# Tokens normalized, turned and copied in two halves, residual sums kept in PSUM, the last up slabs in two strips, in an eight-layer graph and feed-forward kernel

## The chip, the core and the metric

The kernel runs on one core of a Trainium2 chip. The metric is the device time of one execution in microseconds; the time of a kernel is the median of its runs. TensorE (PE) multiplies matrices into PSUM, VectorE (DVE) and ScalarE (ACT) work elementwise, GpSimd (POOL) does small work, and SyncE (SP) issues most of the transfers.

## The reference

128 tokens of 768 float32 values pass through eight layers, each of which adds to x what it computes of the normalized x:

```python
x = x + gnn0(_layernorm(x), src, dst)      # graph attention, two layers
x = x + ffn0(_layernorm(x))                # routed attention, mixing, then a small MLP on a second norm
x = x + gnn1(_layernorm(x), src, dst)
x = x + moe1(_layernorm(x))                # mixture of 8 experts, 2 per token, and a shared one
x = x + gnn2(_layernorm(x), src, dst)       # graph attention with a relu behind it
x = x + moe2(_layernorm(x))                # 8 small experts, all resident
x = x + gnn3(_layernorm(x), src, dst)
x = x + moe3(_layernorm(x))                # mixture of 8 experts, 2 per token
return x

def _layernorm(x, axis=-1, eps=1e-05):
    m = jnp.mean(x, axis=axis, keepdims=True)
    v = jnp.var(x, axis=axis, keepdims=True)
    return (x - m) / jnp.sqrt(v + eps)
```

The lines of the layers are shortened here. One expert is `silu(x @ Wg.T) * (x @ Wu.T) @ Wd.T`.

## The kernel before

All tokens lie on the 128 partitions, so every layer is a sequence of products with the tokens (turned, 128 x 128 a tile, six tiles) as the stationary side, while weights stream past. The weights come as 271 slabs of 128 x 3072 float32 (1.5 MB) through 14 slots; SP issues each slab as its slot's previous one has been used. Each engine has its instructions in an order written out by hand, and semaphores tie them. A queue is worked strictly in order, so a wait holds everything behind it.

Stages in order: `first_wide(0)` and `second(1)` (graph 0), the FFN0 code, `first_narrow(2)` and `second(3)` (graph 1), `mixture(1)`, the attention 2 and its feed-forward, `first_narrow(5)` and `second(6)` (graph 3), `mixture(3)`. Between stages stands a joint; there are nine, with the number `i` of `layernorm`/`layernorm_affine` (L973, L986). Joints 4 and 8 lead into the mixtures, joint 5 out of the first, joint 2 is the second norm within FFN0 (on H1), joints 6 and 7 surround the small experts. A joint runs so:

- TensorE leaves a layer's result in PSUM bank pair AC (768 columns, written as 512 and 256 by `halves()`), and raises x_product.
- VectorE's `take_x` (L1210) adds it to X in SBUF, takes two `bn_stats` of 384 columns, aggregates, adds epsilon; GpSimd (L639) raises to the power -0.5; VectorE normalizes into XN (L979).
- TensorE's `turn` (L1499) transposes six tiles into TP. ScalarE's `transposed` (L677, `transposed_hi` L681) copies 768 columns to XT (or XTh), and the next products start. Where a fp32r split is used, VectorE makes the low part (L1089, L1104).
- `keep_warm(n)` (L1494) is n products of the identity with itself, whose result nobody reads; some stand ahead of each turning.

In `mixture` (L1745 on TensorE), AC is first started with identity times X, so that the experts' results add to it. The router picks experts; VectorE writes their order (L1302), and only then can SP read the numbers of the experts and load their slabs (L576). A pass is a 512-wide slice of one expert (full, split in high and low parts by ScalarE L856 and VectorE L1276) or of two experts side by side (pair, one slab for each side). It does up g (gate), the turning of the pass before, up u, then down of the pass before (L1798, L1851, L1860). The last three passes of mixture 3 (48 to 50) are pairs, as those of mixture 1 (15 to 17). `STRIPS` (L184) loads the down slabs of the last two passes in 2 and 4 strips with a semaphore each. Ahead of g and of u in the last pass stand `keep_warm(14)` (L1930, L1945). At the end VectorE copies X out of AC.

Of the kernel before, what the change touches and what calls it, by code (L numbers as in the profile page):

```python
# [30 lines left out]
E8 = 8  # L31
# [152 lines left out]
STRIPS = {LAST_PASS[l] - back: parts for l in (1, 3) for back, parts in ((1, 2), (0, 4))}  # L184


def strips_of(n):

    l, q, kind, side = WEIGHTS_OF.get(n, (0, 0, "", 0))
    return STRIPS.get(q, 1) if kind == "d" else 1  # L190
# [90 lines left out]
def gnn_ffn_kernel(nc, x_in, edges_in, weights, rows_in, cols_in, small_in, attn_in, ffn0_vectors, l2_terms_in, out):  # L281
    with ExitStack() as ctx:
# [47 lines left out]
        stats = sb("stats", [P, 2, 6])  # L330
# [159 lines left out]

        def group(c, g):
# [46 lines left out]
        def _(sp):  # L538
# [11 lines left out]
            def mixture(l, static_slots, segments, vectors):  # L550
# [3 lines left out]
                for n in range(m["slab"], m["slab"] + 9 * (3 * m["per"]) - (0 if m["shared"] else 3 * m["per"])):  # L554
# [27 lines left out]
                    q, parts = WEIGHTS_OF[n][1], strips_of(n)  # L582
# [3 lines left out]
                    for t in range(parts):  # L586
                        part = slice(t * SLAB // parts, (t + 1) * SLAB // parts)
                        for of, index in closing:
                            sp.dma_start(slab_at(of)[:, part], weights[index, :, part]) \
                                .then_inc(S(f"strip_landed_{q}_{t}"), 16)  # L590
# [83 lines left out]
        def _(act):  # L674
            A = nc.scalar.activation

            def transposed(k):  # L677
                act.wait_ge(S("tr_product"), k + 1)
                A(XT[:].rearrange("p k n -> p (k n)"), TP[:, 0:D], ACT.Copy).then_inc(S("tr_ready"), 1)

            def transposed_hi(k):  # L681

                act.wait_ge(S("tr_product"), k + 1)
                A(XTh[:].rearrange("p k n -> p (k n)"), TP[:, 0:D], ACT.Copy).then_inc(S("tr_ready"), 1)
# [136 lines left out]
            def mixture(l):  # L821
# [38 lines left out]
                A(XTh[:].rearrange("p k n -> p (k n)"), TP[:, 0:D], ACT.Copy).then_inc(S("XTh_ready"), 1)  # L860
# [29 lines left out]
            transposed_hi(0)  # L890
            first_wide(0)
            second(1)

# [8 lines left out]
            act.wait_ge(S("tr_product"), 3)  # L902
            A(MIXT.rearrange("p k n -> p (k n)"), PJ[:, 0:D], ACT.Copy).then_inc(S("mix_ready"), 1)
# [22 lines left out]

            transposed(4)
            first_narrow(2)
            second(3)
            mixture(1)  # L930

            act.wait_ge(S("l2_v_product"), 1)
# [20 lines left out]
            A(CBT[0:E8, :], TP[0:E8, SEG:SEG + P], ACT.Copy).then_inc(S("l2_T_ready"), 1)  # L953

            transposed_hi(8)
            first_narrow(5)
            second(6)
            act.wait_ge(S("graph_used"), GRAPH_HALVES)
# [4 lines left out]
        def _(dve):  # L963
# [9 lines left out]
            def layernorm(i, src, dst, sem=None, count=0):  # L973
# [5 lines left out]
                last = v.tensor_scalar(dst, src, mv[:, 0:1], rstd[:, 0:1], ALU.subtract, ALU.mult)  # L979
                if sem is None:  # L980
                    then(last)
                else:
                    last.then_inc(S(sem), 1)
                    dve.wait_ge(S(sem), count)

            def layernorm_affine(i, src, gain, offset):  # L986

                v.bn_stats(stats[:, 0, :], src[:, 0:384])
                then(v.bn_stats(stats[:, 1, :], src[:, 384:768]))
                then(v.bn_aggr(mv[:], stats[:]))  # L990
                if i == 1:
# [3 lines left out]
                else:  # L995
                    v.tensor_scalar(veps[:, 0:1], mv[:, 1:2], LN_EPS, None, ALU.add).then_inc(S("ln_variance"), 1)
                then(v.scalar_tensor_tensor(XN[:], src, mv[:, 0:1], gain, ALU.subtract, ALU.mult))
                dve.wait_ge(S("ln_rstd"), i + 1)
                v.scalar_tensor_tensor(XN[:], XN[:], rstd[:, 0:1], offset, ALU.mult, ALU.add) \
                    .then_inc(S("tr_input"), 1)  # L1000
# [85 lines left out]
            def transposed_lo(k):  # L1086

                dve.wait_ge(S("tr_ready"), k + 1)
                v.tensor_tensor(XTl[:].rearrange("p k n -> p (k n)"), TP[:, 0:D],  # L1089
                                XTh[:].bitcast(F32).rearrange("p k n -> p (k n)"), ALU.subtract) \  # L1090
                    .then_inc(S("XTl_ready"), 1)
# [8 lines left out]

            def graph_tokens_lo():

                dve.wait_ge(S("tr_ready"), 8)
                v.tensor_tensor(XT_lo.rearrange("p k n -> p (k n)"), TP[:, 0:D],  # L1104
                                XTh[:].bitcast(F32).rearrange("p k n -> p (k n)"), ALU.subtract) \
                    .then_inc(S("graph_tokens_lo"), 1)
# [102 lines left out]

            def take_x(n, add, relu=False):  # L1210

                dve.wait_ge(S("x_product"), n - (n > 4))
                if relu:
                    ins = v.scalar_tensor_tensor(X[:], AC[:, 0:D], 0.0, X[:], ALU.max, ALU.add)
                else:
                    ins = v.tensor_tensor(X[:], AC[:, 0:D], add, ALU.add)
                ins.then_inc(S("x_ready"), 1)
                dve.wait_ge(S("x_ready"), n)
# [1058 lines left out]
```

## Time and profile before

| | us |
|---|---|
| median of 3 runs | 1235.09 (1233.28 to 1235.66) |
| the profiled execution | 1234.37 |
| its span | 1232.4 |
| PE busy | 1169.4 |
| DVE busy | 569.2 |
| ACT busy | 440.3 |
| transfers | 443.15 MB, mean 360 GB/s |

The span runs from the first to the last recorded instruction; the execution's time is a little longer. Busy time of TensorE includes products on constants. The view by stretches gives for each stretch the busy time of each engine, then TensorE's granted clock as a share of full speed, the share in which the DMA engines were busy and what they moved. The timeline lists instructions by start with what ended the idle time before them; the chain lists what the end of the span goes back to. A float32 product appears as two matmul records.

### The profile page before, as it was taken

Reading aid. Unit: us, or ns where it says so; the run is one execution under the profiler, and the core shown is the slowest. Engines: PE = TensorE matmul, PEld = TensorE weight load, DVE = VectorE, ACT = ScalarE, POOL = GpSimd, SP = SyncE. Lnnn points to the kernel's source line nnn. Section 1 sums busy time; section 2 is a strip of 40 time slices with the busy share of each in tenths; the row PEclk is TensorE's granted clock in tenths of the full one; section 3 lists DMA queues with packets and bytes.
Section 4 is the critical chain, followed back from the end, with each engine's and each line's share of the span. In section 5 each row is a group of like instructions: output and inputs, shape, how many; then the busy total and the mean of one; then the engine's idle time right before and its main releaser. Section 6 shows DMA issues by size and latency. Waiting matters only on the chain.

```text
span 1232.4 us, 16004 instructions
## 1 busy us (share of the span) xinstructions
PE 1169.4 (95%) x6537; PEld 744.7 (60%) x6537; DVE 569.2 (46%) x870; ACT 440.3 (36%) x494; POOL 22.0 (2%) x47
## 2 busy tenths in 40 slices
PE   5999999889999999999999999999999999889998
PEld 4677785667855455545866776575565655445543
DVE  6977632337644234301556575463554533233310
ACT  4765512224633223201434345353443422222210
POOL 2000000000000000000000000000000000000000
PEclk9999999999999999999899999999999999999999
DMA  9988645944999999999457498999999999999996
GB/s 376 423 357 346 229 184 208 416 158 190 388 420 424 426 425 426 425 421 420 179 192 277 161 404 307 426 426 426 425 425 425 425 425 426 426 424 424 426 426 247
DMA packets 44647, 443.15 MB, mean 360 GB/s; under 512 B 5008, under 2 KB 5168, under 8 KB 10784
## 3 DMA queue, kind: packets, MB, share of 16 engines
q1 hardware_dynamic: 41760, 427.05, 83.8%
q0 software_dynamic: 2816, 15.09, 3.2%
q8 instruction: 52, 0.85, 0.3%
q14 instruction: 19, 0.16, 0.0%
HBM read 441.73 MB, written 0.39 MB: 359 GB/s over the span
## 4 chain that ended last, share of the span: by engine, by line
PE 78%; DMA 11%; DVE 6%; ACT 3%; issue 1%; POOL 0%; SPq 0%; DVEq 0%; ACTq 0%
PE PJ L1847 17%; DMA scratch<-in_weights 10%; PE PJ L1819 10%; PE AC L1884 8%; PE TP L1906 8%; PE PJ L1828 5%; PE AC L1643 3%; PE MS L1497 3%; PE AC L1655 3%; PE TP L1857 2%; PE PJ L1810 2%; PE PJ L1603 1%; DMA ring<-in_weights 1%; PE PJ L1556 1%; PE PJ L1558 1%
## 5 line engine op out<-in xcount | busy, mean ns | idle before, releaser
L1847 PE MATMUL PJ<-scratch,picked 128*64 128x512 f32 (+1 forms) x564 | 144.5, 595 | 0.5 <-DMA scratch<-in_weights 0.5
L1906 PE MATMUL TP<-ring,extra 128*64 128x512 f32 (+3 forms) x720 | 118.0, 488 | 1.9 <-issue 1.9
L1258 DVE SCALAR_TENSOR_TENSOR act<-low,CB,PJ 128x512 f32<-128x512 f32 x51 | 38.0, 746 | 167.7 <-PE PJ L1847 84.1
L839 ACT ACTIVATE low<-PJ 128x512 f32<-128x512 f32 x51 | 30.2, 592 | 230.0 <-PE PJ L1847 157.6
L1276 DVE TENSOR_TENSOR ring_lo<-ring,w_hi_u 128x1536 fp32r<-128x1536 f32 x46 | 79.6, 1756 | 69.2 <-ACT w_hi_u L856 69.1
L1847 PE MATMUL PJ<-ring,picked 128*32 128x512 f32 (+1 forms) x456 | 101.6, 594 | 0.0
L856 ACT ACTIVATE w_hi_u<-ring 128x1536 fp32r<-128x1536 f32 x46 | 66.9, 1484 | 57.8 <-PE AC L1884 27.1
L1276 DVE TENSOR_TENSOR ring_lo<-ring,w_lo_u 128x1536 fp32r<-128x1536 f32 x40 | 68.9, 1754 | 37.6 <-ACT w_lo_u L856 37.6
L1906 PEld LDWEIGHTS TP<-ring,extra 128*64 128x64 f32 (+1 forms) x720 | 46.7, 126 | 61.5 <-issue 52.9
L1828 PE MATMUL PJ<-ring_lo,XTh 128*128 128x512 f32 x198 | 77.9, 394 | 0.0
L1847 PEld LDWEIGHTS PJ<-scratch,picked 128*64 128x64 f32 (+1 forms) x564 | 42.2, 125 | 55.7 <-issue 55.0
L856 ACT ACTIVATE w_lo_u<-scratch 128x1536 fp32r<-128x1536 f32 x32 | 46.8, 1484 | 77.8 <-DMA scratch<-in_weights 53.0
L856 ACT ACTIVATE w_lo_u<-ring 128x1536 fp32r<-128x1536 f32 x40 | 57.8, 1483 | 31.7 <-PE AC L1884 19.4
L1497 PE MATMUL MS<-ident 128*128 128x128 f32 x566 | 68.8, 276 | 0.0
L1497 PEld LDWEIGHTS MS<-ident 128*128 128x128 f32 x566 | 66.1, 192 | 2.5 <-issue 2.1
L1819 PE MATMUL PJ<-w_lo_u,extra_lo 128*128 128x512 f32 x150 | 61.0, 407 | 0.0
L1819 PE MATMUL PJ<-w_hi_u,extra_lo 128*128 128x512 f32 x150 | 59.3, 406 | 1.2 <-DVE ring_lo L1276 1.2
L1819 PE MATMUL PJ<-w_lo_u,XTh 128*128 128x512 f32 x150 | 59.0, 393 | 0.0
L1819 PE MATMUL PJ<-w_hi_u,XTh 128*128 128x512 f32 x150 | 59.0, 393 | 0.0
L1847 PE MATMUL PJ<-extra,picked 128*64 128x512 f32 (+1 forms) x132 | 58.6, 593 | 0.1
L1847 PEld LDWEIGHTS PJ<-ring,picked 128*32 128x32 f32 (+1 forms) x456 | 29.3, 120 | 43.4 <-issue 42.5
L1884 PE MATMUL AC<-w_hi_u,extra_lo 128*128 128x512 f32 x208 | 50.1, 355 | 4.9 <-DVE extra_lo L1284 4.9
(440 smaller groups left out, 2087.2 us busy)
## 6 DMA issues: line engine op xcount, KB each, us to landing
ring<-in_weights SPq DMA_DIRECT2D x162, 1536.0 KB, 17.6
scratch<-in_weights SPq DMA_DIRECT2D x78, 1536.0 KB, 20.4
extra<-in_weights SPq DMA_DIRECT2D x23, 1536.0 KB, 20.2
extra<-in_attn POOLq DMA_DIRECT2D x11, 768.0 KB, 8.7
scratch<-in_weights SPq DMA_DIRECT2D x12, 384.0 KB, 17.5
extra<-in_attn POOLq DMA_DIRECT2D x6, 512.0 KB, 9.2
extra<-in_weights SPq DMA_DIRECT2D x4, 768.0 KB, 29.3
scratch<-in_ffn_vectors POOLq DMA_DIRECT2D x1, 2688.5 KB, 12.4
```

The source lines that it names most:

```text
L839: A(silu, PJ[:, 0:SEG], ACT.Silu).then_inc(S("silu_ready"), 1)
L856: A(hi_half(n, half), half_slab(n, half), ACT.Copy).then_inc(S("whole_hi"), 1)
L1258: v.scalar_tensor_tensor(hexp, silu, weight, PJ[:, SEG:2 * SEG], ALU.mult, ALU.mult) \
L1276: v.tensor_tensor(slab_lo(n)[:, half * HALF:(half + 1) * HALF], half_slab(n, half), hi_half(n, half).bitcast(F32), ALU.subtract).then_inc( ...
L1497: mm(dst, ident[:], ident[:], start=True, stop=True)
L1643: ins = mm(AC[:, a:b], act1T[:, j % 2, t * P:(t + 1) * P], slab_at(n)[:, t * D + a:t * D + b], start=(j == 0 and t == 0), stop=(j == last ...
L1655: ins = mm(AC[:, a:b], x[:, t * P:(t + 1) * P], w[:, t % 2 * D + a:t % 2 * D + b], start=(j == 0 and t == 0 and x is xl), stop=False, skip ...
L1819: return mm(dst, x[:, t, :], hi_half(n, t // 3)[:, t % 3 * SEG:(t % 3 + 1) * SEG], start=start, stop=stop)
L1828: mm(dst, XTh[:, t, :], slab_lo(n)[:, t * SEG:(t + 1) * SEG], start=(apart and t == 0), stop=False)
L1847: ins = mm(dst[c], x[:, t, c], slab_at(LOAD[q, kind, side])[:, t * SEG:(t + 1) * SEG], start=(t == 0), stop=(t == KT - 1))
L1884: ins = mm(AC[:, a:b], x[:, t * P:(t + 1) * P], w[:, a:b], start=False, stop=(q == end and t == 3 and w is hi and x is hTh), skip_group_ch ...
L1906: ins = mm(Y[c, a:b], hT_of(q)[:, t * P:(t + 1) * P][:, c], slab_at(LOAD[q, "d", side])[:, t * D + a:t * D + b], start=(j == j0 and t == 0 ...
```

## The change

- The layer's sum is made in PSUM: TensorE adds X (and H1 in FFN0) to AC by products with the identity (`add_tokens`), in place of some of the products on constants; VectorE's `take_x` goes, except the one with relu in joint 6 (count 5). ScalarE copies the sum back to X (`keep_x`), after the statistics of the columns have been taken.
- VectorE reads the statistics from AC, three of 256 columns; the first two after the first half of the last product (semaphore x_half).
- Normalization, turning and copy go in two halves of 384 columns; the second half of the turned tokens lies in its own bank (from column 512). Consumers start on tr_early and wait for tr_ready at their fourth tile. The low parts follow in halves too.
- In the mixtures the separate start of AC by identity times X goes, since the sum is still there; 14 constants stand ahead of the turning where 5 and 7 stood.
- In the last pass of each mixture the two `keep_warm(14)` go, and the two u slabs are loaded in two strips; the up products wait for a strip at tile 0 and 3.

Core of the diff:

```diff
-STRIPS = {LAST_PASS[l] - back: parts for l in (1, 3) for back, parts in ((1, 2), (0, 4))}
+STRIPS = {(LAST_PASS[l] - back, kind): parts for l in (1, 3) for back, kind, parts in ((0, "u", 2), (1, "d", 2), (0, "d", 4))}
...
+            def transposed(k, out=XT[:]):
+
+                for half, (product, ready) in enumerate((("tr_first", "tr_early"), ("tr_product", "tr_ready"))):
+                    act.wait_ge(S(product), k + 1)
+                    A(tiles(out, half), TP[:, half * SEG:half * SEG + D // 2], ACT.Copy).then_inc(S(ready), 1)
+
+            def keep_x(n):
+
+                for i, (a, b) in enumerate(halves()):
+                    act.wait_ge(S("x_stats"), 2 * (n - (n > 4)) - 1 + i)
+                    ins = A(X[:, a:b], AC[:, a:b], ACT.Copy)
+                ins.then_inc(S("x_ready"), 1)
...
+            def stats_of_sum(n):
+
+                if n == 4:
+                    dve.wait_ge(S("closing_added"), 1)
+                else:
+                    dve.wait_ge(S("x_half"), n - (n > 4) - (n > 5))
+                at, steps = D // 3, 2 * (n - (n > 4))
+                v.bn_stats(stats[:, 0, :], AC[:, 0:at])
+                v.bn_stats(stats[:, 1, :], AC[:, at:2 * at]).then_inc(S("x_stats"), 1)
+                if n == 4:
+                    dve.wait_ge(S("pair_added"), 3)
+                else:
+                    dve.wait_ge(S("x_product"), n - (n > 4))
+                v.bn_stats(stats[:, 2, :], AC[:, 2 * at:3 * at]).then_inc(S("x_stats"), 1)
+                dve.wait_ge(S("x_stats"), steps)
                 then(v.bn_aggr(mv[:], stats[:]))
...
+                if kept:
+                    dve.wait_ge(S("x_ready"), kept)
+                for name, a, b in (("tr_half", 0, D // 2), ("tr_input", D // 2, D)):
+                    v.tensor_scalar(XN[:, a:b], src[:, a:b], mv[:, 0:1], rstd[:, 0:1], ALU.subtract, ALU.mult) \
+                        .then_inc(S(name), 1)
...
             def turn(k, src, warm=0, dst=TP):
 
                 keep_warm(warm)
-                pe.wait_ge(S("tr_input"), k + 1)
-                for t in range(KT):
-                    ins = nc.tensor.transpose(dst[:, t * P:(t + 1) * P], src[:, t * P:(t + 1) * P], ident[:])
-                ins.then_inc(S("tr_product"), 1)
+                for half, (given, product) in enumerate((("tr_half", "tr_first"), ("tr_input", "tr_product"))):
+                    pe.wait_ge(S(given), k + 1)
+                    for t in range(3):
+                        at = half * 3 + t
+                        ins = nc.tensor.transpose(dst[:, half * SEG + t * P:half * SEG + (t + 1) * P],
+                                                  src[:, at * P:(at + 1) * P], ident[:])
+                    ins.then_inc(S(product), 1)
...
+            def add_tokens(start=False):
+
+                for a, b in halves():
+                    mm(AC[:, a:b], ident[:], X[:, a:b], start=start, stop=False, skip_group_check=True)
+
             def second(c, n):
...
-                keep_warm(10)
+                if c == 1:
+                    pe.wait_ge(S("x_loaded"), 16)
+                else:
+                    pe.wait_ge(S("x_ready"), {3: 2, 6: 6}[c])
+                add_tokens()
+                keep_warm(4)
                 turn_attention(c, 0)
                 pe.wait_ge(S("attn_ready"), GROUP_BASE[c] + 1)
-                for a, b in halves():
-                    ins = mm(AC[:, a:b], attn_tile(c)[:, 0:P], hs2[:, a:b], start=False, stop=True,
-                             skip_group_check=True)
-                ins.then_inc(S("x_product"), 1)
+                for name, (a, b) in zip(("x_half", "x_product"), halves()):
+                    mm(AC[:, a:b], attn_tile(c)[:, 0:P], hs2[:, a:b], start=False, stop=True,
+                       skip_group_check=True).then_inc(S(name), 1)
...
-                keep_warm(5)
+                turn(k, XN, warm=14)
                 pe.wait_ge(S("x_ready"), {1: 3, 3: 7}[l])
-                for a, b in halves():
-                    mm(AC[:, a:b], ident[:], X[:, a:b], start=True, stop=False, skip_group_check=True)
-                turn(k, XN, warm=7)
                 keep_warm(4)
-                pe.wait_ge(S("tr_ready"), k)
+                pe.wait_ge(S("tr_early"), k)
...
+                        if (q, kind) in STRIPS and t % 3 == 0:
+                            pe.wait_ge(S(f"strip_landed_{kind}_{end - q}_{t // 3}"), 32 * (nth + 1))
...
-                    if q == end:
-                        keep_warm(14)
                     up("g", q, count_chosen if q == first else None)
...
-                    if q == end:
-                        keep_warm(14)
                     up("u", q)
...
-            turn(3, XN, warm=18)
-            pe.wait_ge(S("tr_ready"), 3)
+            add_tokens()
+            pe.wait_ge(S("h1_ready"), 1)
+            for a, b in halves():
+                mm(AC[:, a:b], ident[:], H1[:, a:b], start=False, stop=False, skip_group_check=True)
+            turn(3, XN, warm=6)
+            pe.wait_ge(S("tr_early"), 3)
...
-                keep_warm(5, AC[:, 0:P])
+            pe.wait_ge(S("x_ready"), 5)
+            add_tokens(start=True)
```

## Rows read from the trace of the kernel before

**Rows 1.** The page's chain of work that ended last, by engine.
```profile
PE 78%; DMA 11%; DVE 6%; ACT 3%; issue 1%; POOL 0%; SPq 0%; DVEq 0%; ACTq 0%
```

**Rows 2.** Stretches: busy us of each engine, TensorE's granted clock, DMA share, GB/s.
```profile
280.00:300.00 20.00, 19.99 (x98) 13.62 (x97) 15.91 (x46) 6.34 (x7) 0.26 (x1) 1.00 0.27 100
...
610.00:616.00 6.00, 6.00 (x18) 4.34 (x18) 3.35 (x10) 5.98 (x5) 0.00 (x0) 0.50 0.00 0
...
820.00:900.00 80.00, 80.00 (x395) 50.09 (x394) 41.51 (x30) 35.20 (x32) 0.00 (x0) 1.00 1.01 426
```

**Rows 3.** Timeline of joint 4: start us, length, engine, line, idle before.
```profile
275.42 2.85 ACT L856 ACTIVATE w_hi_u<-scratch 128x1536 fp32r<-128x1536 f32 x2
...
277.17 0.96 DVE L1216 TENSOR_TENSOR extra<-AC,extra 128x768 f32<-128x768 f32 x1 [2.72 <-PE AC L1741]
278.16 0.56 DVE L974 BATCH_NORM_STATS2 stats<-extra 128x6 f32<-128x384 f32 x1
...
278.18 1.56 PE L1752 MATMUL AC<-extra,ident 128*128 128x512 f32 x4
...
280.29 0.68 DVE L979 TENSOR_SCALAR extra<-extra,mv,rstd 128x768 f32<-128x768 f32 x1 [0.68 <-POOL rstd L639]
...
281.13 0.82 PE L1504 MATMUL TP<-ident,extra 128*128 128x128 f32 x6
...
281.99 0.81 ACT L679 ACTIVATE extra<-TP 128x768 f32<-128x768 f32 x1 [3.73 <-PE TP L1504]
...
282.85 1.51 PE L1758 MATMUL MS<-small,extra 128*128 128x8 f32 x12
```

**Rows 4.** Chain of waits, joints 1 to 3: start us, length, what.
```profile
167.22 7.14 PE MS L1497 x64
...
220.89 1.52 PE MS L2077 x12
...
222.85 1.57 PE AC L2082 x4
...
228.36 0.89 PE TP L1504 x6
...
230.14 4.99 PE PJ L1546 x11
```

**Rows 5.** Timeline, constants ahead of joint 2's turning.
```profile
214.60 4.29 PE L1497 MATMUL MS<-ident 128*128 128x128 f32 x36
```

**Rows 6.** Timeline of joint 6: the turning, and the wide products.
```profile
607.76 0.88 PE L1504 MATMUL TP<-ident,extra 128*128 128x128 f32 x6 [0.50 <-DVE extra L979]
...
612.85 6.06 PE L2134 MATMUL PJ<-ring,extra 128*128 128x384 f32 x12
```

**Rows 7.** Chain of waits over the span, the mixtures' last passes.
```profile
489.00 4.39 PE AC L1884 x24
...
512.80 35.24 DMA scratch<-in_weights
...
554.24 3.13 PE MS L1497 x28
...
1175.26 6.00 PE AC L1884 x24
...
1197.61 3.32 PE MS L1497 x28
...
1206.82 3.13 PE MS L1497 x28
...
1216.82 10.06 PE TP L1906 x60
```

**Rows 8.** Timeline of TensorE at 1175 us.
```profile
1175.26 0.62 PE L1884 MATMUL AC<-w_hi_u,extra_lo 128*128 128x512 f32 x2 [1.82 <-DVE extra_lo L1284]
```

**Rows 9.** The weight stream's last two issues (us) and their time to landing.
```profile
L589 SPq DMA_DIRECT2D scratch<-in_weights x2: 1445/1462/1480, 1206.2 to 1207.9; - x2
...
DMA to landing us min/median/max: 13.3/13.8/14.3
```

More of the change, by code:

```diff
@@ L901, in _ @@
             A(Q, TP[:, 0:D // 4], ACT.Copy).then_inc(S("q_copied"), 1)
-            act.wait_ge(S("tr_product"), 3)
-            A(MIXT.rearrange("p k n -> p (k n)"), PJ[:, 0:D], ACT.Copy).then_inc(S("mix_ready"), 1)
+            for half, name in enumerate(("tr_first", "tr_product")):
+                act.wait_ge(S(name), 3)
+                ins = A(tiles(MIXT, half), PJ[:, half * SEG:half * SEG + D // 2], ACT.Copy)
+            ins.then_inc(S("mix_ready"), 1)
             act.wait_ge(S("v_product"), 1)
@@ L991, in layernorm_affine @@
+                dve.wait_ge(S("tr_half"), count)
+                dve.wait_ge(S("tr_input"), count)
+            def layernorm_affine(i, src, gain, offset, kept=None):
+                if kept:
+                    stats_of_sum(kept)
+                else:
+                    stats_of(src)
                 if i == 1:
@@ L1084, in edge_masks, with transposed_lo @@
                 then(v.tensor_scalar(maskb[:], maskb[:], NOT_AN_EDGE, None, ALU.subtract))
[L1086 to L1091, printed above, removed]
+            def transposed_lo(k, out, sem):
+                for half, name in enumerate(("tr_early", "tr_ready")):
+                    dve.wait_ge(S(name), k)
+                    ins = v.tensor_tensor(tiles(out, half), TP[:, half * SEG:half * SEG + D // 2],
+                                          tiles(XTh[:].bitcast(F32), half), ALU.subtract)
+                ins.then_inc(S(sem), 1)
             def graph_split_lo(s, both=(0, 1)):
@@ L1208, in second @@
                 weights_of(c, 0)
[L1210 to L1218, printed above, removed]
             def ahead(values):
@@ L1466, in _ @@
             weights_of(4, 2)
-            take_x(5, None, relu=True)
-            layernorm(6, X[:], XN[:], "tr_input", 8)
+            dve.wait_ge(S("x_product"), 4)
+            dve.wait_ge(S("x_ready"), 4)
+            v.scalar_tensor_tensor(X[:], AC[:, 0:D], 0.0, X[:], ALU.max, ALU.add).then_inc(S("x_ready"), 1)
+            dve.wait_ge(S("x_ready"), 5)
+            layernorm(6, X[:], 8)
             dve.wait_ge(S("l2_gate_product"), 1)
@@ L1527, in project @@
                             pe.wait_ge(S("graph_lo"), 2 * s + t // 3 + 1)
+                        if j == 0 and t == 3:
+                            pe.wait_ge(S("tr_ready"), 8)
                         if j:
@@ L1841, in up @@
                     for side in range(sides(q)):
-                        landed(pe, LOAD[q, kind, side])
+                        if (q, kind) not in STRIPS:
+                            landed(pe, LOAD[q, kind, side])
                     pe.wait_ge(S("gathered"), base + a + 1)
@@ L2080, in _ @@
             pe.wait_ge(S("f_ready"), 1)
-            for a, b in halves():
-                ins = mm(AC[:, a:b], FT[0:F0, :], w_tile(31, a, b)[0:F0], start=False, stop=True,
-                         skip_group_check=True)
-            ins.then_inc(S("x_product"), 1)
+            for name, (a, b) in zip(("x_half", "x_product"), halves()):
+                mm(AC[:, a:b], FT[0:F0, :], w_tile(31, a, b)[0:F0], start=False, stop=True,
+                   skip_group_check=True).then_inc(S(name), 1)
             turn(4, XN, warm=15)
-            pe.wait_ge(S("tr_ready"), 4)
+            pe.wait_ge(S("tr_early"), 4)
+            pe.wait_ge(S("x_ready"), 2)
             first_narrow(2)
@@ L2145, in _ @@
             pe.wait_ge(S("l2_T_ready"), 2)
-            for a, b in halves():
-                mm(AC[:, a:b], CBT[0:E8, :], slab_at(n)[0:E8, L2_W + a:L2_W + b], start=True, stop=False,
+            for name, (a, b) in zip(("x_half", "x_product"), halves()):
+                mm(AC[:, a:b], CBT[0:E8, :], slab_at(n)[0:E8, L2_W + a:L2_W + b], start=False, stop=False,
                    skip_group_check=True)
```

135 lines of the change are left out of this document (72 added, 63 removed).

## The prediction

> **What bounds the kernel now.** I read the page first: the chain of work that ended last is 78% TensorE, 11% DMA, 6% VectorE, 3% ScalarE [rows 1]. So the time is TensorE's queue plus the places where it waits. Next, the stretches: at 280 to 300 us, where the experts are being chosen, the DMA engines are busy 0.27 of the time; inside a mixture (820 to 900) they run at 1.01 and 426 GB/s [rows 2]. A mixture is thus a transfer stream that starts when the order of the experts is known and from then on has a length of its own (one slab of 1.573 MB is 3.69 us at 426 GB/s). Whatever ends earlier ahead of the choice moves this stream, and what follows, earlier by as much. So savings ahead of the mixtures add up, and they aren't hidden under the DMA's 360 GB/s mean.
>
> Then one joint (where a sum becomes the next normalized, turned tokens), in the order of time. Before the first mixture: the products end about 277.13; VectorE's addition 277.17 to 278.13; statistics from 278.16; the normalization 280.29, 0.68 long; transposes 281.13; ScalarE's copy 281.99, 0.81 long; router products 282.85 [rows 3]. That is 5.7 us, with nine such places (numbered 0 to 8). TensorE fills them with products on constants, 0.223 us each (7.14 us for 32) [rows 4].
>
> **The change, part by part.** I cost each joint as the later of two queues: VectorE's and the one TensorE works through.
>
> *VectorE.* The addition (0.96) goes; the sum is finished by TensorE from an identity product on X. Three statistics of 256 columns read PSUM, the first two during TensorE's second half. The nearest row is 0.56 for 384 from SBUF [rows 3]: 0.35 apiece is taken; bounds are 0.25 and 0.56. The third ends 0.7 after the products. From the start of the old statistics to the normalization were 2.13, of which two statistics took 1.03, leaving 1.10 for aggregate, variance and GpSimd's power [rows 3]. So: 277.13+0.7+1.10 = 278.95, and the first half normalized (0.40, bounds 0.34 and 0.68) at 279.4, against 280.97. ScalarE copies X into SBUF meanwhile (0.81 for 768 columns by its copy [rows 3]; two pieces, some 1.0), done by 278.4, so the new wait of the normalization on X is covered by GpSimd; uncovered it would cost up to 0.8.
>
> *TensorE.* In front of the transposes of a mixture stood 5 constants, 4 token passes (1.56 [rows 3]) and 7 constants; now 14 constants: 3.12 from 277.13, 280.2 instead of 281.1. TensorE's queue, not VectorE, then ends last.
>
> *Halves of turning and copy.* Old: transposes' start to consumer 1.78 (228.36 to 230.14) [rows 4]. New: three transposes (half of 0.7, plus 0.2 to drain), half a copy (0.45, bounds 0.41 and 0.6), about 1.1: a gain of 0.65. The second half is needed three matmuls later and arrives about then.
>
> The joints:
> - 0: nothing; the splitting of the first two slabs, which wait for transfers, follows anyway.
> - 1: 32 constants, 7.14 us [rows 4], stay and end after VectorE: 0.2, from the copy alone (three constants stay behind the turning).
> - 2 (H1): VectorE reads SBUF as before. TensorE had 18 constants, 4.29 [rows 5]; now 4 token passes, 4 passes on H1 and 6 constants: 3.0+1.3 = 4.3, no change. The halves give 0.9 at the product of 220.89 [rows 4]; behind it ScalarE's table load takes part back: 0.8.
> - 3: 15 constants after the products of 222.85 to 224.42 end at 227.7 in today's times; the turning began at 228.36 [rows 4]. TensorE becomes last: 0.65, and 0.65 for halves: 1.3.
> - 4 and 8: 0.9 by the queue. The halves give nothing here: ScalarE must first copy X, then do the split of slab g (2.85, today done at 275.42 to 278.27 before the copy is wanted [rows 3]); now it ends 278.4+2.85 = 281.25, half a copy 281.8. TensorE's transposes and 4 constants end 281.9. Router at 281.9 instead of 282.85: 0.95 each. Were ScalarE's cover gone, 0.1 to 0.5 of it.
> - 5: 15 constants bind before and after: 0.7 from halves.
> - 6: addition with relu unchanged; the turning began 607.76 after 0.50 idle [rows 6], so halves give 0.3+0.7 less 0.2 for the token passes (they take the place of 5 constants): 0.8. After it the granted clock is 0.50 over 610 to 616, 1.2 GHz, and the 12 passes at 612.85 take 6.06 [rows 2, 6]; full speed would be about two thirds. The idle ahead of it shrinks, and if the clock holds, up to 2.0 more (beyond that ScalarE's splits and table load bind). Bounds 0.8 and 2.8; 1.5 taken.
> - 7: as 3, 1.35.
>
> *Last passes.* Today: 14 constants, g, turning, 14 constants, u, in mixture 3 at 1197.61 (3.32) and 1206.82 (3.13) [rows 7]. How late is the DMA? The last strip is issued at 1207.9 and lands 13.3 later, 1221.2 [rows 9]. Six slabs back (u, d, d, two sides each) at 3.69 is 1199.1: g has landed then. Without constants g starts near 1199.4, u at 1205.3 (its first strip is in at 1202.8, its second 1206.5, needed 1207.9; unstripped it would wait for 1206.5), the two downs 1.55 after u's end (measured today: 1206.82+3.13+5.3 to 1216.82), and the last quarter near 1221.2, just as its strip lands. End about 1222.8 against 1226.88: 4.1, and no more, since the transfer now binds. The strips cost some more DMA issues on SP, and the first u strip waits for two free slots instead of one; transfers then stand queued for over 13 us [rows 9], which hides it.
>
> Against this stands the clock. TensorE is idle from 1197.6 to 1199.4. The product at 1175.26 also followed 1.82 us idle [rows 8] and its 24 passes took 6.00 where 4.39 is usual [rows 7]: 1.6 lost. The Trainium skill ("TensorE: Matmul & The Clock Gate", on HAM oscillation) says that waits for transfers put the engine back to half clock and the next products run cold, a rule against removing these constants. By that rule, the trace agrees at 1175.26, and the end gains 2.4; without it 4.1. From the two rows alone, the price of a gap as long as 1.8 us is 1.6, so 4.1-1.7 = 2.4 is taken, with 4.1 as the upper bound. In mixture 1 g waits for the transfer of 512.80+35.24 = 548.04 [rows 7], so the first 14 constants lay in a wait: removing them gives nothing and leaves 3.7 us idle, so the 1.6 to 1.7 is lost; the second 14 (3.13 at 554.24 [rows 7]) are saved: 1.4. Bounds 1.0 and 2.8 (the last strip binds).
>
> Sum: 0.2+0.8+1.3+0.95+1.4+0.7+1.5+1.35+0.95+2.4 = 11.55. The profiled execution has a span of 1232.4 and a time of 1234.37: 1220.85 and 1222.8. The median of the runs, 1235.09, lies 0.7 above that execution: 1223.5.
>
> **The rivals.**
> - *The clock holds* in joint 6 and after both waits: 1.3+1.4+1.7 more, 1219.1. For it: 1.82 us idle is close to the new gap. Against: 3.7 idle in mixture 1. Chance 0.16.
> - *The halves don't do what they say*: TensorE takes up the consumer only as the second half arrives, or ScalarE's added copy and doubled instruction overhead (bounds 0.6 and 0.56 above) eat them. Joints 1, 2, 3, 5, 6 and 7 then lose 0.2+0.8+0.65+0.7+0.8+0.65 = 3.8: 1227.3. For it: several joints hang on TensorE's queue. Chance 0.14.
> - *The streams don't move*: if the mixtures' transfers were held by slots and not by the choice of experts, only 1.4+2.4 and joints 5 to 7 in part remain, about 6: 1229. The idle DMA at 280 to 300 speaks against. Chance 0.04.
> - *Slower:* the clock falls in the thinned joints. Constants in `second` go from 10 to 4, before the H1 turning from 18 to 6. Joint 6 shows the price: 6 us at 0.50 [rows 2], 3.0 lost. From four such places on the gain is gone; with five (two routers, FFN0, two of `second`) it is 1223.5+15.0 = 1238.5. Against: constants are replaced by other products, and idle time shrinks. Chance 0.03.
>
> **How the numbers follow.** Forecast 1223.5 with chance 0.63; rivals 0.16, 0.14, 0.04, 0.03. Unknown prices (statistics, half copies: nine joints by 0.2 either way) give 2 us around each. 8 in 10 takes in the clock's rival on one side and the halves' on the other: 1218.5 to 1229. 0.2% is 2.5 us, about what can be told from no change. Faster 0.94, same 0.03, slower 0.03.
>
> **What would show it.** Right: router products about 4.7 instead of 5.7 after the last attention product; three statistics reading PSUM near 0.42 each; turning directly behind the constants in joints 3, 4, 7, 8; both mixtures' streams 3 and 9 us earlier; g of the last pass behind a DMA wait, at a clock of 0.50; last strip landing as the last quarter begins. Wrong: statistics over 0.6; the normalization waiting for ScalarE's X; the low clock in new places; u waiting for its second strip.

## The result, and the profile after

The changed kernel takes 1220.36 us (median of 4 runs, 1218.92 to 1221.46) beside 1234.29 us for the kernel before (4 runs on the same chip, 1233.28 to 1235.66): a ratio of 0.989, 95% interval 0.9875 to 0.9906. Forecast were 1223.5 us and a range of 1218.5 to 1229. The profiled execution has a time of 1220.83 us and a span of 1219.1 us, against 1232.4 before.

The page's chain by engine, to be held against [rows 1]: TensorE's part is smaller, the transfers' larger, VectorE's smaller, and SyncE's queue has entered with the strips.

```profile
PE 76%; DMA 12%; DVE 5%; ACT 3%; SPq 2%; issue 1%; POOL 0%; DVEq 0%; ACTq 0%
```

Timeline of joint 4, the answer to [rows 3] (start us, length us, engine, line, operation, idle time before it):

```profile
272.75 1.56 PE L1789 MATMUL AC<-extra 128*128 128x512 f32 x4 [0.37 <-ACT extra L737]
273.91 0.43 DVE L1007 BATCH_NORM_STATS2 stats<-AC 128x6 f32<-128x256 f32 x1 [2.25 <-PE AC L1789]
...
274.59 0.42 DVE L1013 BATCH_NORM_STATS2 stats<-AC 128x6 f32<-128x256 f32 x1
274.71 0.87 ACT L695 ACTIVATE extra<-AC 128x512 f32<-128x512 f32 x2 [2.01 <-DVE stats L1008]
...
275.47 2.86 ACT L868 ACTIVATE w_hi_u<-scratch 128x1536 fp32r<-128x1536 f32 x2
...
276.15 0.87 DVE L1027 TENSOR_SCALAR extra<-extra,mv,rstd 128x384 f32<-128x384 f32 x2 [0.68 <-POOL rstd L647]
...
277.27 0.82 PE L1537 MATMUL TP<-ident,extra 128*128 128x128 f32 x6
...
278.21 0.87 ACT L689 ACTIVATE extra<-TP 128x384 f32<-128x384 f32 x2
278.82 1.45 PE L1804 MATMUL MS<-small,extra 128*128 128x8 f32 x12
```

The three statistics take 0.43, 0.41 and 0.42 us and read PSUM; the first two start while the products (272.75 to 274.31) still run, the third 0.28 us behind them. ScalarE copies X at 274.71, splits slab g from 275.47 on (2.86 us) and only then, at 278.21, copies the turned tokens, as forecast. The router products follow the attention product by 6.07 us; before it was 7.28 (275.57 to 282.85).

Chain of waits in joints 2 and 3 (start us, length us, what), against [rows 4] and [rows 5]:

```profile
215.45 1.29 PE AC L2125 x4
216.74 1.34 PE MS L1528 x12
218.07 1.02 PE TP L1537 x6
...
219.63 1.28 ACT L941
...
221.34 1.55 PE AC L2136 x4
222.90 3.54 PE MS L1528 x30
226.44 0.34 PE TP L1537 x3
226.80 0.50 ACT extra L689
...
227.35 4.99 PE PJ L1584 x11
```

In joint 3 the turning stands directly behind the constants, the consumer waits for a copy of 0.50 us, and it starts at 227.35 instead of 230.14. ScalarE's table load (1.28 us) is now on the chain of joint 2, as the prediction said.

Chain of waits, the mixtures' last passes, against [rows 7]:

```profile
508.96 34.48 DMA scratch<-in_weights
...
543.69 7.07 PE PJ L1896 x24
...
551.34 5.33 PE PJ L1896 x24
...
558.22 10.18 PE TP L1955 x60
...
1130.26 29.85 DMA scratch<-in_weights
...
1199.18 13.21 DMA scratch<-in_weights
...
1212.43 1.10 PE TP L1955 x4
...
1214.40 1.11 PE AC L2013 x2
```

In mixture 1, g runs cold (in part at half clock) as forecast: 7.07 us instead of 5.37. The chain there goes through g, but the last strip landed at 567.25 just as the down products reached it (they take 10.18 us; 10.06 without any wait), so two limits ended within 0.1 us of each other. At the end of the kernel the last strip lands at 1212.39 and the last quarter of the down products starts on it: the transfer sets the end.

**Where the time went.** I took from the timelines the starts of the same product in both kernels, so that each stretch between two of them is one joint (from the last product of the sum to the first product on the turned tokens; in joint 2, whose table load lies behind that first product, to the next one, L2082 before and L2136 after) or one end of a mixture. All in us:

| place | before | after | gain | forecast |
|---|---|---|---|---|
| ahead of joint 1 | 165.66 | 165.44 | 0.22 | 0 |
| joint 1 | 10.26 | 9.87 | 0.39 | 0.2 |
| joint 2 | 10.25 | 9.45 | 0.80 | 0.8 |
| joint 3 | 7.29 | 6.01 | 1.28 | 1.3 |
| joint 4 | 7.28 | 6.07 | 1.21 | 0.95 |
| mixture 1, router to closing add | 292.32 | 290.44 | 1.88 | 1.4 |
| joint 5 | 6.92 | 6.12 | 0.80 | 0.7 |
| joint 6 | 6.98 | 6.13 | 0.85 | 0.8 |
| behind joint 6, to the first product of joint 7's sum | 11.82 | 9.55 | 2.27 | 0.7 |
| joint 7 | 11.64 | 10.24 | 1.40 | 1.35 |
| joint 8 | 7.28 | 6.07 | 1.21 | 0.95 |
| mixture 3, router to closing add | 530.52 | 529.59 | 0.93 | 2.4 |

With 0.10 in the stretches between, the closing add of the whole kernel comes 13.34 us earlier (1227.74 to 1214.40). The forecast had 11.55. In joint 2 the gain up to the first product (L2131) is 1.04; the table load takes 0.24 of it back.

### The profile page after: what moved, and what is told of

Read it like the earlier page. It is cut to its first block, busy times and chain, and to the rows that moved or that the text cites. A ratio compares the mean times of both kernels' runs of the same rounds, so it can differ in the third digit from the quotient of the medians.

```text
span 1219.1 us, 15740 instructions
## 1 busy us (share of the span) xinstructions
PE 1153.8 (95%) x6379; PEld 726.4 (60%) x6379; DVE 564.7 (46%) x880; ACT 446.2 (37%) x516; POOL 21.9 (2%) x47
## 4 chain that ended last, share of the span: by engine, by line
PE 76%; DMA 12%; DVE 5%; ACT 3%; SPq 2%; issue 1%; POOL 0%; DVEq 0%; ACTq 0%
PE PJ L1896 16%; DMA scratch<-in_weights 11%; PE PJ L1865 10%; PE AC L1933 8%; PE TP L1955 7%; PE PJ L1874 5%; PE AC L1681 3%; PE AC L1693 3%; PE MS L1528 3%; PE PJ L1856 2%; SPq L597 2%; PE TP L1906 2%; PE PJ L1641 1%; DMA ring<-in_weights 1%; PE PJ L1594 1%
## 5 line engine op out<-in xcount | busy, mean ns | idle before, releaser
L1933 PE MATMUL AC<-w_lo_u,extra_lo 128*128 128x512 f32 x192 | 46.4, 355 | 7.4 <-DVE extra_lo L1318 7.4
L868 ACT ACTIVATE w_hi_u<-scratch 128x1536 fp32r<-128x1536 f32 x20 | 28.7, 1481 | 66.3 <-DMA scratch<-in_weights 64.3
```

Of the source, the lines that this page charges most:

```text
L868: A(hi_half(n, half), half_slab(n, half), ACT.Copy).then_inc(S("whole_hi"), 1)
L1933: ins = mm(AC[:, a:b], x[:, t * P:(t + 1) * P], w[:, a:b], start=False, stop=(q == end and t == 3 and w is hi and x is hTh), skip_group_ch ...
```

## The experiments

Times are medians. To make different chips comparable I count each kernel's gain against the kernel before of its own comparison: 13.9 for the changed kernel, 14.9 for its repetition.

### The last passes alone, and undone

The kernel before with only the last passes changed:

```diff
                 for q in range(first, end + 1):
-                    if q == end:
-                        keep_warm(14)
                     up("g", q, count_chosen if q == first else None)
...
-                    if q == end:
-                        keep_warm(14)
                     up("u", q)
```

(and `STRIPS` with its waits as in the change).

> The kernel before with the change of the last passes alone: the 28 products on constants of each mixture's last pass gone, the up slabs there in two strips; tokens, sums and turning as before. The prediction gave this part 1.4 us in mixture 1 and 2.4 us at the end, with a loss to the clock of 1.7 in each: 3.8 in all, 1230.5. What the trace of the changed kernel suggests: mixture 1 gives 1.9 and the end 3.8 to 4.1, because no clock is lost in the last one and the landing of the last strip sets the end: 5.9, 1228.4. Third: the transfers bind already without this part and less than 2 comes of it, over 1232.

Measured: 1228.78 against 1234.72, ratio 0.9953 (0.9939 to 0.9967), a gain of 5.9, as read from the traces and 2.1 more than the prediction's 3.8. The reverse, the changed kernel with both groups of 14 back (the same lines with + for -):

> The changed kernel with the two groups of 14 constants put back ahead of g and u of each mixture's last pass; the strips of the up slabs stay. The counterpart of the first run. If the parts of the change add up, it loses what the first run gains: 3.8 by the prediction (1224.2), 5.9 by the traces (1226.3). If the last passes hang on the transfers alone, it loses under 2 (1222). The second 14 are expected on the path in both mixtures (3.1 each), the first 14 inside the wait for the g slab.

Measured: 1224.74 against 1234.72, 0.9925 (0.9911 to 0.9938): a gain of 10.0, so 4 to 5 us lost, between the prediction's 3.8 and the 5.9 of the first run. And the constants back in mixture 3 only (`if q == end and l == 3`):

> The changed kernel with the 28 constants back in the last pass of mixture 3 only. The prediction gave the end 2.4 (clock lost on g): 1222.8. The traces say that the clock holds on g there and that the last strip's landing sets the end, some 3.4 to 3.9 lost with the constants: 1224. Rival: the end hangs on the transfer with or without them, under 1: 1221.

Measured: 1223.13 beside 1219.4 for the unaltered kernel on the same chip: 3.7 lost, between the forecast's 2.4 and its bound of 4.1. The stretch from router to closing add of mixture 3 is 530.24 with the constants and 527.54 without them in the two traces, 2.7. Over all 13 traces it is 530.24 to 531.99 in the five kernels with these constants and 526.76 to 529.59 in the eight without: the two groups do not overlap, and their means differ by 2.9.

### Up slabs whole

```diff
-STRIPS = {(LAST_PASS[l] - back, kind): parts for l in (1, 3) for back, kind, parts in ((0, "u", 2), (1, "d", 2), (0, "d", 4))}
+STRIPS = {(LAST_PASS[l] - back, kind): parts for l in (1, 3) for back, kind, parts in ((1, "d", 2), (0, "d", 4))}
```

> The changed kernel with the up slabs of the last passes loaded whole, so that u waits for both slabs and not for their first halves; no constants there, the down slabs in strips as before. The prediction: unstripped, u would wait 1.2 us longer in each mixture, of which the last one's is hidden behind the last strip's landing: 1.2 slower at most, 1220.4 to 1221.6. Rival: the strips carry the last passes' gain: u starts 2 us and more later in both mixtures, 1223 or more. Third: more transfers in smaller pieces cost the stream something, and whole slabs are faster by 0.5 or more.

Measured: 1222.75 against 1234.72, 0.9903 (0.989 to 0.9917), a gain of 12.0: 2 to 3 less than the changed kernel, more than the 1.2 expected at most, with intervals that overlap. The trace assigns little of it to the strips. In mixture 1 u waited for nothing; the mixture took 291.01, beside 290.44 to 290.88 in seven of the eight other traces without the second 14 constants (the eighth has 292.46). In mixture 3 u did wait for its second slab:

```profile
1198.17 5.37 PE L1896 MATMUL PJ<-ring,extra 128*64 128x512 f32 x24 [1.43 <-DMA ring<-in_weights]
```

and the closing add came 2.83 us behind the last landing instead of 2.01, so some 0.8 is the price of the whole slabs there, hidden in the scatter of the stretch (527.40). Joint 7 took 11.89 and the stretch behind it was 1.4 longer, in code that is the same in both kernels. That led to the repetition below.

### Halves undone

```diff
-                for half, (given, product) in enumerate((("tr_half", "tr_first"), ("tr_input", "tr_product"))):
-                    pe.wait_ge(S(given), k + 1)
+                pe.wait_ge(S("tr_input"), k + 1)
+                for half, product in enumerate(("tr_first", "tr_product")):
...
-                for half, (product, ready) in enumerate((("tr_first", "tr_early"), ("tr_product", "tr_ready"))):
-                    act.wait_ge(S(product), k + 1)
-                    A(tiles(out, half), TP[:, half * SEG:half * SEG + D // 2], ACT.Copy).then_inc(S(ready), 1)
+                act.wait_ge(S("tr_product"), k + 1)
+                A(out.rearrange("p (h k) n -> p h (k n)", h=2), turned_halves(TP), ACT.Copy) \
+                    .then_inc(S("tr_ready"), 1)
```

(the normalizations in one instruction each.)

> The changed kernel with normalization, turning and ScalarE's copy of the tokens in one piece each (the copy of X and the sums in PSUM stay). The prediction gave the halves 3.8 us over the joints 1, 2, 3, 5, 6 and 7 and nothing in joints 4 and 8: 1224.2. Rival, the halves don't pay (ScalarE's second instruction and its overhead eat them): within 0.8 of the changed kernel, 1220.4 to 1221.2. If they pay in the joints 4 and 8 too, 1225.5.

Measured: 1226.6 against 1234.72, 0.9942 (0.9929 to 0.9956), a gain of 8.1, so 5.8 to 6.8 lost, more than any of the expectations. Then the sums alone, that is this kernel with the constants of the last passes back and whole up slabs:

> The changed kernel with everything but the sums undone: normalization, turning and copy in one piece, the 28 constants of both last passes back, the up slabs whole. What is left of the change: X added by TensorE, statistics read from PSUM, ScalarE's copy of X, the token passes in place of constants. The prediction gives this part 0.65 (joint 3), 0.95 (4), 0.7 (7), 0.95 (8), less 0.2 in joint 6 and with up to 1.5 from a shorter idle there: 3.1 to 4.6, 1229.7 to 1231.2. Rival, the copies of X and the PSUM reads cost what the addition saved: 1234 and more. By what is left after the runs on the other two parts (6 for the halves, 6 for the last passes, of 14.5 in all): 2.5, 1231.8.

Measured: 1230.51 against 1234.96, 0.9969 (0.9954 to 0.9983), a gain of 4.4. The joints in the traces settle what each part is worth; the two kernels agree in each to 0.01 us:

| joint | 1 | 2 | 3 | 4 | 5 | 6 | 7 | 8 | sum of gains |
|---|---|---|---|---|---|---|---|---|---|
| before | 10.26 | 10.25 | 7.29 | 7.28 | 6.92 | 6.98 | 11.64 | 7.28 | |
| sums only | 10.32 | 10.31 | 6.71 | 6.33 | 6.83 | 7.04 | 10.94 | 6.33 | 3.09 |
| sums and halves | 9.87 | 9.45 | 6.01 | 6.07 | 6.12 | 6.13 | 10.24 | 6.07 | 4.85 more |

The rival that halves don't pay is out: they pay 0.26 even in joints 4 and 8, where I had given them nothing. But 0.39 of joint 6's 0.91 goes again behind it: with the clock at full, the stretch there takes 9.55 us with halves and 9.16 with whole turning. What the timed loss has beyond the joints is not all explained; the trace of the whole turning lost 1.63 between joints 5 and 6 (22.30 for 20.67) to a low clock at 580 to 584 us, in code that is the same in both kernels.

### The changed kernel again

> The changed kernel once more, unaltered, beside the next three. Theory, from the runs so far: a single execution has two sources of its own scatter. One, TensorE's clock falls to 0.50 or holds in joint 6 (at 613 us it fell in the first and third run, not in the changed kernel's execution with the same code up to there), worth some 1.6 to 2 us upstream of mixture 3. Two, mixture 3's slabs land up to 2.3 us later against their issue in some executions, at the same rate in GB/s. So this one's trace should differ from the first of the same kernel in at least one of the two, with a time between 1218.5 and 1222.5. Rival: both are fixed by the code, and this trace repeats the first: no low clock between 570 and 690 us, span 1219.1 within 0.5.

Measured: 1219.4 (1218.48 to 1221.44), 0.9886 (0.987 to 0.9902). Its joints repeat the first trace to 0.01 us, all of them. Two things don't. First the clock. Stretches with TensorE's granted clock (the first of the three numbers at the end; DMA share and GB/s follow), of the repetition:

```profile
604.00:608.00 4.00, 4.00 (x8) 2.22 (x8) 3.54 (x10) 4.00 (x4) 0.00 (x0) 0.57 0.00 0
...
641.00:644.00 3.00, 3.00 (x14) 2.42 (x14) 2.83 (x10) 2.97 (x5) 0.53 (x1) 1.00 0.99 421
```

of the changed kernel's first trace:

```profile
604.00:608.00 4.00, 4.00 (x14) 2.41 (x14) 3.79 (x9) 3.98 (x4) 0.00 (x0) 1.00 0.00 0
```

and of the kernel with whole up slabs:

```profile
604.00:608.00 4.00, 4.00 (x16) 2.57 (x16) 3.15 (x9) 4.00 (x4) 0.00 (x0) 1.00 0.00 0
610.00:616.00 6.00, 5.00 (x16) 2.58 (x16) 3.90 (x3) 1.04 (x3) 0.00 (x0) 0.79 0.59 242
...
641.00:644.00 3.00, 3.00 (x8) 2.01 (x7) 2.35 (x10) 1.92 (x4) 0.00 (x0) 0.50 0.92 389
```

The same instructions between 570 and 690 us, and the clock fell to half (1.2 GHz) at 604, not at all, or at 613 and 641. The price by the stretches above: 0.66 (10.21 for 9.55), nothing, or 1.65 and 1.4. Two more traces have the same code there: that with both groups of constants back had no low clock, that with the constants back in mixture 3 only fell at 613 and 641 us.

Second, the landing of slabs. The same slab of mixture 3, issued 134.7 to 134.8 us behind the router product each time, in the kernel before (issued at 832.0), the changed kernel (819.5), its repetition (820.6), in this order, issue to landing:

```profile
DMA to landing us min/median/max: 14.4/14.4/14.4
```

```profile
DMA to landing us min/median/max: 16.7/16.7/16.7
```

```profile
DMA to landing us min/median/max: 14.8/14.8/14.8
```

The first trace of the changed kernel drew the good clock and the late landings, which partly cancel.

### Fewer constants, and constants in the waits

```diff
-            turn(1, XN, warm=32)
+            turn(1, XN, warm=20)
...
-            turn(4, XN, warm=15)
+            turn(4, XN, warm=11)
...
-            keep_warm(15, PJ[:, 0:P])
+            keep_warm(11, PJ[:, 0:P])
             turn(6, XN)
...
-            turn(8, XN, warm=15)
+            turn(8, XN, warm=11)
```

> The changed kernel with fewer products on constants ahead of four turnings: 20 for 32 in joint 1, 11 for 15 in joints 3, 5 and 7. In its trace the first half of the normalized tokens is ready 3.0 us (joint 1) and 1.07 us (the others) before the transposes start. If TensorE's queue binds these joints, as the prediction says, it saves 2.7+3x0.89 = 5.3: 1215.1. Rival, the clock: with less work there it falls after the joints, 1.6 and more each, and from four such falls on nothing is gained: 1221 or more. Second rival: what follows joint 1 hangs on VectorE and ScalarE (their work for the router of the first mixture), so joint 1 gives 1 at most: 1217.

Measured: 1217.11 (1213.12 to 1217.9), 0.9854 (0.9836 to 0.9872), 2.3 less than the unaltered kernel beside it. The joints gave exactly what TensorE's queue says: joint 1 2.67 (9.86 to 7.19), joint 3 0.90, joint 5 0.90, joint 7 0.89, together 5.36. The trace shows where the rest went: low clock at 601 (0.65) and 635 (1.4), and mixture 1 at 292.46, 1.9 longer. Its chain there:

```profile
541.54 7.91 PE PJ L1896 x24
...
556.91 10.06 PE TP L1955 x60
```

Half of the 1.9 is the transfers' (the last strip landed 0.93 later behind the router than in the repetition), half the cold g: no strip stops the down products, and they end 0.92 later than the strip asks.

```diff
+                    if q == end and l == 1:
+                        keep_warm(14)
                     up("g", q, count_chosen if q == first else None)
...
-            turn(7, XN, warm=15)
+            turn(7, XN, warm=17)
...
+            keep_warm(4, TP[:, 0:P])
             pe.wait_ge(S("l2_weighted"), 1)
```

> The changed kernel with products on constants only where TensorE waits anyway: 14 ahead of g of the last pass of mixture 1 (not of mixture 3), 2 more ahead of joint 6's turning, 4 ahead of the turning of the experts' results behind it. Theory, the low clock is a cost of its own: g of mixture 1 takes 5.3 and not 7.07 us and the clock holds at 613 us, 1.7 always and 1.6 in the executions in which it fell: 1.7 to 3.3 faster, 1217.1 to 1218.7. Rival: the constants run into the arrival of the slab or of the tokens and cost what the clock gives, 1220.4.

Measured: 1219.55 (1219.25 to 1221.3), 0.989 (0.9875 to 0.9905): no gain, where 1.7 to 3.3 were expected. The clock does hold, at 540 to 550 and between 570 and 690 us, but mixture 1 takes 290.57 with a warm g and 290.44 with a cold one. The chain of this kernel says why: it ends in the strip, as the last mixture does.

```profile
554.13 14.39 DMA scratch<-in_weights
...
568.57 1.10 PE TP L1955 x4
```

A cold g hides behind the last strip's transfer as far as that transfer reaches. The closing add stands 2.01 us behind the strip's landing in the repetition (warm g) and in the first trace (cold g); in the run with fewer constants, with a g of 7.91 us, it stood 2.93 behind. Both edits together, with three more constants ahead of the first terms behind joint 7:

```diff
+                        if n > 2 and t == 1:
+                            keep_warm(3)
                         term_rows(c, t - 1)
```

> Both edits of the two runs before together: fewer constants where the tokens are ready early (20 for 32 in joint 1, 11 for 15 in joints 3, 5 and 7), and constants in the waits (14 ahead of g in mixture 1's last pass, 2 ahead of joint 6's turning, 4 ahead of the turning of the experts' results, 3 ahead of the first turning of terms behind joint 7, where the clock had fallen at 635 to 641 us in three runs). Theory: fewer constants save 5.3 and lost 3 of it in the executions in which the clock fell in joints 6 and 7 (three of five, 1217.1 to 1217.9, against 1213.1 and 1214.1 in the others); filled, all executions lie with the fast two: 1213.5. Rival, the clock falls elsewhere or the filling delays the path: 1217. Low clock between 570 and 690 us in the trace would speak for the rival.

Measured: 1214.14 (1212.35 to 1215.9), 0.9829 (0.9814 to 0.9844), a gain of 20.8 over the kernel before and the fastest version here. Its trace has no low clock between 50 and 1036 us. The median is near the expected 1213.5, but not all executions came down to the fast two of the run with fewer constants (1213.12 and 1214.08): three of six lie at 1214.7 to 1215.9.

### The idle ahead of joint 6, in the kernel before

```diff
-            turn(7, XN, warm=15)
+            turn(7, XN, warm=18)
```

> The kernel before with 3 more constants ahead of joint 6's turning (18 for 15), which closes the 0.50 us idle there. The prediction took the low clock at 610 to 616 us for a consequence of that idle and priced it at up to 2.0 us. If so, the clock holds there, and the wide product starts the next products 1.5 to 2.3 us earlier: 1232.0 to 1232.8. If the clock falls a few us later instead, as in the first run (613 us), 1.5 come of it in joint 6 and nothing if the later products pay: 1232.8 to 1234.3. Rival, the idle has no part in it and the dip stays at 610: 1234.3 and the low clock unchanged.

Measured: 1232.98 against 1234.96, 0.9985 (0.9974 to 0.9997), 2.0 faster. Stretches of this kernel and its wide products, against [rows 2] and [rows 6]:

```profile
610.00:616.00 6.00, 6.00 (x28) 4.19 (x29) 4.09 (x10) 5.98 (x5) 0.00 (x0) 1.00 0.00 0
620.00:624.00 4.00, 4.00 (x6) 1.63 (x6) 1.02 (x1) 0.00 (x0) 0.00 (x0) 0.57 0.31 132
```

```profile
611.85 4.14 PE L2134 MATMUL PJ<-ring,extra 128*128 128x384 f32 x12
```

The wide products take 4.14 instead of 6.06 us and the stretch behind joint 6 9.16 instead of 11.82; then the clock falls at 620, and joint 7 takes 13.34 instead of 11.64: 1.0 of 2.7 us is kept in this trace. Whether the filled idle moved the fall isn't shown by one trace. The kernel with the last passes alone has the code of the kernel before here, idle unfilled, and its clock fell at 583 and 613 us instead of 610, so the place changes without the filling too. For the filling speaks the timed difference, whose interval (0.4 to 3.2 us) just leaves out zero.

## Why the prediction was right, point by point

- *VectorE's and TensorE's queues in the joints.* Right. All eight joints (joint 6 without what follows it) lie within 0.3 us of their terms, and sum to 7.94 against 7.05. Split by the runs: sums 3.09 (forecast 3.25), halves 4.85 (forecast 3.8). The steps that were short are "the halves give nothing here", of joints 4 and 8 (0.26 each), and the 0.2 for joint 1 (0.45). TensorE's queue does bind in joints 4 and 8 (the router products of 278.82 follow the 4 constants of 277.92 without a gap), but a copy in one piece behind ScalarE's split would have ended 0.26 later than these constants.
- *TensorE's queue binds joints 3, 5 and 7.* Shown: fewer constants gave 0.9 in each, to 0.01 us what was taken away. In joint 1 too: 12 constants fewer gave 2.67 us, all of their length. The prediction let them stay and put no price on it.
- *End of mixture 1.* Direction right, size 1.9 for 1.4, and the reason was partly wrong. I subtracted 1.7 for a cold g. Warm or cold, the mixture can end at the same time (290.57 and 290.61 warm, 290.44 cold), because the last strip's landing binds, which I had named only as the upper bound. Not always: with fewer constants, g took 7.91 us and 0.9 of it showed.
- *Joint 6 and its clock.* The mis-sized term: 3.1 for 1.5, above even the bound of 2.8. The bounds of 0.8 and 2.8 stood for the two outcomes, and I took a value between; in this execution the clock held, and it gave 2.3 instead of the 2.0 that I had at most. The repetition shows that either can happen: it had the clock at 0.57 over 604 to 608 and lost 0.66. That the idle ahead of the turning has a part in it is likely from the timed filled kernel before, but not shown; that it doesn't decide alone is shown by the falls that differ with the same code.
- *The last passes of mixture 3.* 0.9 in this pair, 3.7 in the timed pair, forecast 2.4. Both steps of my sum, 4.1 and 1.7, were off. First, the 4.1: I took the last strip to land 13.3 us behind its issue, but of the two transfers of [rows 9] the first took 13.3 and the last 14.3, so it landed at 1222.17. From that landing to the closing add were 5.57 us in the kernel before and are 2.01 in the changed one: 3.56 was to be had, and the run with only these constants back gave 3.7. In this pair the last strip landed 2.63 us later behind the router product (527.58 for 524.95), and 3.56 - 2.63 is the 0.93 of the table. Second, the 1.7 for the clock: the forecast put g behind a wait and cold; it waited 2.03 us (1.82 had been followed by a fall [rows 8]) and ran warm, in 5.37 us:

```profile
1189.88 5.37 PE L1896 MATMUL PJ<-ring,extra 128*64 128x512 f32 x24 [2.03 <-DMA ring<-in_weights]
```

 Of the eight traces without constants there, seven had g warm behind 2.03 to 2.18 us of idle; that of the whole turning had it cold behind 2.20:

```profile
1193.47 7.07 PE L1892 MATMUL PJ<-ring,extra 128*64 128x512 f32 x24 [2.20 <-DMA ring<-in_weights]
```

 Even 2.91 us of idle ahead of g of mixture 1 were followed by 5.37 us in the repetition, and 2.49 by 7.07 in the first trace. So the price of a gap of some 2 us isn't the fixed 1.6 that I read from two rows. The Trainium skill ("TensorE: Matmul & The Clock Gate", on HAM oscillation) says that waits for transfers, if long enough, put the engine back to half clock, so that the next products run cold; the traces show that for several waits here and not for each, and the row that I called agreement, 1175.26, was a wait for VectorE and not for a transfer. The late landings of this execution show earlier in the stream too: the first slab that mixture 3 waits for landed 9.8 us earlier (1046.60 to 1036.83), not the 12.4 by which its stream started earlier, and 2.3 of the difference appear at the slab above (16.7 for 14.4).
- *The streams move.* Right: 4.0 us earlier at the first mixture's router (forecast 3) and 12.4 at the second's (forecast 9), the same 134.7 us to the issue of the slab above, and 426 GB/s over 820 to 900 us in both. The slower rival (clock lost in five thinned joints) did not occur; the rival "the clock holds" (1219.1) is nearer to the median of 1220.4 than my forecast; in the first trace the clock held in two of its three places, joint 6 and g of mixture 3, and fell in mixture 1.
- *The total.* 13.3 for 11.55, and that it is this near is in part luck: the joints, mixture 1 and the clock behind joint 6 gave 2.9 more than forecast, and the end gave 1.5 less, where late landings outweighed a clock that held.

What stays open: why a slab's landing lags. It is the same queue, order, rate and distance from the router; in 13 traces the slab landed 13.7 to 14.8 us after issue in nine and 15.5 to 16.7 in four. A part of the 16 DMA engines running behind would fit the tail of the changed kernel (their busy share falls from 0.51 to 0.05 between 1207 and 1212 us, with the last strips outstanding), but no run here tested it. What the up strips are worth is not settled either: one trace shows 0.8 us at the end of mixture 3, and the timed difference of 2 to 3 has the clock's scatter in it. And no run shows what makes the clock fall in one execution and hold in the next.

## What to carry to other kernels

- Time a chain of joints by the distance between two products on the same engine. It repeats to 0.01 us where whole executions scatter by 3, as long as the clock doesn't fall inside the joint (joint 7: 10.24 us, and 11.89 with a fall), and it shows which part of a change pays where. Look at the stretch behind the joint too: 0.39 of what joint 6 gained was lost there.
- Constants that keep an engine warm are dead weight where they outlast what they wait for: compare the end of the constants with the moment the tokens are ready. Take the surplus away and put some into real idle time; here the one edit alone gave 2.3, the other nothing, both together some 6 to 7 (20.8 against 13.9 and 14.9, each over the kernel before).
- Before pricing a cold product, ask whether the next thing on the path waits for a transfer anyway. If it does, the clock costs only what outlasts that transfer: nothing for a g of 7.07 us here, 0.9 for one of 7.91.

## What the runs showed of the hardware that I had not expected

- The clock's fall is not fixed by the program. With the same instructions it fell at 604 us, at 613 and 641 us, or not between 570 and 690 us, at costs of 0.66, 3.1 and 0 us; idle of 2.49 us was followed by half clock and idle of 2.91 us at the same place by full clock, idle of 2.20 us by half clock and idle of 2.03 to 2.18 us at the same place by full clock.
- Landings of the same slab differ by up to 3 us between executions (13.7 to 16.7 us from issue) at an unchanged 426 GB/s. In a kernel that ends on a transfer this shows in the time.
- The second transfer that SyncE issues lands between 14.2 and 15.4 us after the start, and what follows starts earlier or later too: in the changed kernel it landed at 14.2 and the first product of joint 1 stands at 165.44 us, with filled waits at 15.4 and 166.62 us.
